# A recurrence step: its cube taken from a scaled copy, and one add moved from VectorE to GpSimd

## The reference, cut to what matters

```
# layer 1, one GRU step
r = sigmoid(i_r + h_r); z = sigmoid(i_z + h_z)          # i = x @ W_ih, h_ = h @ W_hh
n = tanh(i_n + r * h_n)
h = (1 - z) * n + z * h
# layer 2, one step of four Runge-Kutta stages, driven by x + h
dq = q - q**3 / 3 - p + drive + tanh(q) @ coupling.T + bias
dp = EPSILON * (q + ALPHA - BETA * p)
# stages at q, q + DT/2*dq1, q + DT/2*dq2, q + DT*dq3; then
q = clip(q + DT/6 * (dq1 + 2*dq2 + 2*dq3 + dq4)); p = clip(...)
```

## Time and profile before

| | |
|---|---|
| median of 3 runs | 3523.38 us (3521.14 to 3523.52) |
| the profiled execution | 3529.05 us, span 3527.2 us |
| PE busy, PEld busy | 3439.5 us, 3178.9 us |
| DVE busy | 2816.7 us (80%) |
| ACT busy | 2605.1 us (74%) |
| POOL busy | 1478.5 us (42%) |
| granted clock of TensorE, mean over the span | 0.987 of full speed |

### The profile page before, as it was taken

How to read it: one execution, slowest core, us unless ns; L and a number is a source line. 1 busy time by engine, 2 the same in 40 slices (tenths; PEclk the granted TensorE clock), 3 DMA queues, 4 the chain that set the end, 5 groups by cost and what they waited for, 6 DMA issues and landing times.

```text
span 3527.2 us, 296053 instructions
## 1 busy us (share of the span) xinstructions
PE 3439.5 (98%) x115469; PEld 3178.9 (90%) x115469; DVE 2816.7 (80%) x20699; ACT 2605.1 (74%) x23713; POOL 1478.5 (42%) x6169
## 2 busy tenths in 40 slices
PE   8989999999999999999999999999999999999978
PEld 4479999999999999999999999999999999999954
DVE  2068888888888888888888888888888888888876
ACT  3257777777777777777777777777777777777752
POOL 0024444444444444444444444444444444444421
PEclk9999999999999999999999999999999999999978
DMA  3000000000000000000000000000000000000001
GB/s 131 24 26 1 1 1 1 1 1 1 1 1 1 1 1 1 1 1 1 1 1 1 1 1 1 1 1 1 1 1 1 1 1 1 1 1 1 1 2 48
DMA packets 9433, 24.29 MB, mean 7 GB/s; under 512 B 556, under 2 KB 600, under 8 KB 8792
## 3 DMA queue, kind: packets, MB, share of 16 engines
q1 hardware_dynamic: 8832, 19.92, 1.6%
q10 hardware_dynamic: 88, 0.02, 0.0%
HBM read 15.75 MB, written 4.19 MB: 6 GB/s over the span
## 4 chain that ended last, share of the span: by engine, by line
PE 85%; DVE 7%; ACT 6%; issue 2%; DMA 0%; ACTq 0%; DVEq 0%; POOL 0%; POOLq 0%
PE psum L1187 46%; PE psum L1144 32%; PE psum L1114 5%; ACT tpart L583 2%; PE psum L1290 1%; ACT tfull L585 1%; DVE psum L895 1%; DVE tpart L852 1%; ACT qterm L558 1%; ACT pterm L554 1%; DVE psum L875 1%; DVE qnext L895 1%; DVE psum L887 0%; ACT qterm L547 0%; DVE wih L981 0%
## 5 line engine op out<-in xcount | busy, mean ns | idle before, releaser
L1187 PE MATMUL psum<-tpart,cpl 128*128 128x32 f16 (+1 forms) x65536 | 1966.8, 176 | 21.1 <-DVE tpart L852 14.5
L1187 PEld LDWEIGHTS psum<-tpart,cpl 128*128 128x128 f16 x65536 | 1781.8, 96 | 113.0 <-DVE tpart L852 22.8
L1144 PE MATMUL psum<-hpart,whh 128*128 128x32 f16 x49152 | 1553.3, 177 | 15.9 <-DVE hpart L828 12.0
L1144 PEld LDWEIGHTS psum<-hpart,whh 128*128 128x128 f16 x49152 | 1374.4, 96 | 38.3 <-DVE hpart L828 14.2
L852 DVE TENSOR_TENSOR tpart<-tfull,tpart 128x8 f16<-128x8 f32 x4096 | 682.1, 167 | 154.0 <-ACT tfull L585 11.4
L895 DVE TENSOR_REDUCE psum<-psum 128x8 f32<-128x24 f32 x3072 | 574.8, 188 | 110.1 <-PE psum L1187 3.7
L583 ACT ACTIVATE tpart<-psum 128x8 f16<-128x8 f32 x3072 | 527.3, 172 | 90.5 <-DVE psum L895 18.4
L585 ACT ACTIVATE tfull<-psum 128x8 f32<-128x8 f32 x3072 | 526.4, 172 | 0.0
L583 ACT ACTIVATE tpart<-qnext 128x8 f16<-128x8 f32 x1024 | 213.5, 208 | 312.4 <-DVE qnext L895 312.4
L505 ACT ACTIVATE rz<-gates 128x16 f32<-128x16 f32 x1024 | 241.1, 235 | 267.5 <-DVE gates L787 267.0
L547 ACT ACTIVATE qterm<-psum 128x16 f32<-128x16 f32 x3072 | 413.6, 202 | 0.0
(11 more groups left out here) (153 smaller groups left out, 4449.8 us busy)
## 6 DMA issues: line engine op xcount, KB each, us to landing
xrow<-in_x_dram SPq DMA_DIRECT2D x4, 1024.0 KB, 11.7
out_dram<-space SPq DMA_DIRECT2D x16, 256.0 KB, 2.0
wih<-in_L_cond_W_ih_dram SPq DMA_DIRECT2D x3, 1024.0 KB, 10.2
space<-in_L_cond_W_hh_dram SPq DMA_DIRECT2D x1, 3072.0 KB, 19.1
space<-in_L_cond_coupling_dram SPq DMA_DIRECT2D x1, 1024.0 KB, 19.3
xrow<-in_cond_dram SPq DMA_DIRECT2D x1, 1024.0 KB, 4.7
wih<-in_L_cond_Wk_dram SPq DMA_DIRECT2D x1, 1024.0 KB, 5.7
wih<-in_L_cond_Wo_dram SPq DMA_DIRECT2D x1, 1024.0 KB, 7.9
```

The lines of the kernel that those rows point to most:

```text
L1144: mm = pe.matmul(gate_out[x][:, :, :, c * B:(c + 1) * B], whh[:, w, k, n * P:(n + 1) * P], copies_in(hpart[:, k, :, :]), start=(c == 0 and ...
L1187: mm = pe.matmul(stage_out[a][:, 0:reps, :, col:col + B], cpl[:, w, k, n * P:(n + 1) * P], copies_in(tpart[:, s % 2, k, :, :])[:, 0:reps, ...
```

## The change

Two things are changed.

1. In stages 1 to 3 the cube's factor q is no longer read from the argument `qt` in PSUM but from one of ScalarE's scaled copies of it in `qterm` (the copy with index COPY_OF); the scale is divided out in `base`. ScalarE makes that copy first, then the square, then the other copies. The reduce that overwrites `qt` in stages 1 and 2 gets a wait for the last of the copies. Stage 0's cubic loses its wait for q1, which an earlier instruction on VectorE has already awaited.
2. `new_h_full` leaves VectorE. GpSimd makes the same add in `whole_h`: half 0 after `next_x1` and before `next_uhat`, half 1 between `pn` and `phat`. `h_low` on VectorE waits for it through `hs_ready`. On VectorE `sum_gates(1)` is moved ahead of `base(2)`.

```diff
--- before.py
+++ after.py
@@ -58,6 +58,9 @@
             lin((-1, p3), (1 / DT, q[0])),
             lin((-1, p4), (-2 / DT, q[0]), (2 / DT, q[1]), (4 / DT, q[2])),
             pn]
+
+
+COPY_OF = [2, 3, 3]
 
 
 HALVES = 2
@@ -377,11 +380,24 @@
                 pool.tensor_tensor(kept[:, x, :], rz[:, x, HC:2 * HC], hs[:, (v - 1) % 2, x * HC:(x + 1) * HC],
                                    ALU.mult).then_inc(kept_ready[x], 1)
 
+            def whole_h(x, v):
+
+                pool.wait_ge(fresh_ready[x], v)
+                pool.wait_ge(kept_ready[x], v)
+                if v > 2:
+                    pool.wait_ge(h_ready, v - 2)
+                if v > 1:
+                    pool.wait_ge(h_parts[x], v)
+                pool.tensor_tensor(hs[:, v % 2, x * HC:(x + 1) * HC], fresh[:, x, :], kept[:, x, :],
+                                   ALU.add).then_inc(hs_ready[x], 1)
+
             for x in range(HALVES):
                 keep_part(x, 1)
+                whole_h(x, 1)
             next_x1(1, 0)
             for x in range(HALVES):
                 keep_part(x, 2)
+                whole_h(x, 2)
             next_uhat(1)
             first_drive(1)
 
@@ -408,6 +424,8 @@
                                        ALU.add).then_inc(sums_ready[s], 1)
                     if s == 1 and tail <= T:
                         next_x1(tail, now)
+                        if gru <= T:
+                            whole_h(0, gru)
                         next_uhat(tail)
                     if s == 2 and gru <= T:
                         keep_part(1, gru)
@@ -416,6 +434,8 @@
                     pool.wait_ge(qterm_ready[3], now)
                     pool.wait_ge(sums_ready[2], now)
                     pool.tensor_tensor(pn[:, :], sums[:, 3, :], qterm[:, 3, 3, :], ALU.add).then_inc(pn_ready, 1)
+                    if gru <= T:
+                        whole_h(1, gru)
                     pool.wait_ge(pn_ready, now)
                     pool.tensor_scalar(phat[:, :], pn[:, :], clampc[:, 0:1], clampc[:, 1:2],
                                        ALU.min, ALU.max).then_inc(phat_ready, 1)
@@ -541,11 +561,12 @@
 
             sums_of = recovery_sums()
 
-            def stage_terms(s):
-
-                for r in range(s + 1, 4):
+            def stage_terms(s, rs):
+
+                for r in rs:
                     ins = act.activation(in_halves(qterm[:, s + 1, r, :]), qt, ACT.Copy, scale=STEP[s] * sums_of[r][s + 2])
-                ins.then_inc(qterm_ready[s + 1], 1)
+                    if r == s + 1:
+                        ins.then_inc(qterm_ready[s + 1], 1)
 
             def first_terms(v):
 
@@ -589,11 +610,13 @@
                         if s == 2 and a == 0 and gru <= T:
                             scaled_omz(1, gru)
                     if s < 3:
-                        stage_terms(s)
+                        stage_terms(s, [COPY_OF[s]])
                     arg, s_next = (in_halves(qnext[:, :]), 0) if s == 3 else (qt, s + 1)
                     if s < 3 or tail <= T:
                         act.activation(in_halves(sq[:, s_next, :]), arg, ACT.Square,
                                        scale=k_stage[s]).then_inc(sq_ready[s_next], 1)
+                    if s < 2:
+                        stage_terms(s, [r for r in range(3, s, -1) if r != COPY_OF[s]])
                     if s == 0:
                         if t >= 1:
                             plain_q(t - 1)
@@ -814,12 +837,6 @@
                     dve.tensor_tensor(part_of(x, 0), in_k(fresh[:, x, :]), in_k(kept[:, x, :]),
                                       ALU.add).then_inc(hi_ready[x], 1)
 
-            def new_h_full(x, v):
-
-                if v > 2:
-                    dve.wait_ge(h_ready, v - 2)
-                dve.tensor_tensor(hs_of(x, v), fresh[:, x, :], kept[:, x, :], ALU.add).then_inc(hs_ready[x], 1)
-
             def h_low(x, v):
 
                 if v > 0:
@@ -843,7 +860,6 @@
                 for x in range(HALVES):
                     weigh(x, v)
                     new_high(x, v)
-                    new_h_full(x, v)
                     h_low(x, v)
 
             def split_tanh(s, a, v, ready, n):
@@ -867,13 +883,14 @@
 
                 if s == 0:
                     dve.wait_ge(sq_ready[0], v - 1)
-                    dve.wait_ge(q1_ready, v)
                     dve.scalar_tensor_tensor(cub, sq[:, 0, :], CLAMP * CLAMP, q1[:, :], ALU.min, ALU.mult).then_inc(cub_ready, 1)
                 else:
 
                     dve.wait_ge(sq_ready[s], v)
-                    dve.scalar_tensor_tensor(in_halves(cub), in_halves(sq[:, s, :]), LINEAR[s], qt,
+                    dve.scalar_tensor_tensor(cub, sq[:, s, :], LINEAR[s], qterm[:, s, COPY_OF[s - 1], :],
                                              ALU.add, ALU.mult).then_inc(cub_ready, 1)
+
+            sums_of = recovery_sums()
 
             def base(s, v):
 
@@ -884,7 +901,8 @@
                                              ALU.mult, ALU.add).then_inc(base_ready, 1)
                 else:
                     dve.wait_ge(sums_ready[s - 1], v)
-                    dve.scalar_tensor_tensor(stage_base, in_halves(cub), -STEP[s - 1] / 3, in_halves(sums[:, s - 1, :]),
+                    dve.scalar_tensor_tensor(stage_base, in_halves(cub), -1 / (3 * sums_of[COPY_OF[s - 1]][s + 1]),
+                                             in_halves(sums[:, s - 1, :]),
                                              ALU.mult, ALU.add).then_inc(base_ready, 1)
 
             def sum_stage(s, a, v):
@@ -892,6 +910,8 @@
                 dve.wait_ge(stage_mm[s][a], v)
                 if a == 0:
                     dve.wait_ge(base_ready, stage_count(s, v))
+                    if s in (1, 2):
+                        dve.wait_ge(qterm_ready[s], v)
                 dve.tensor_reduce(qt[:, a, :] if s < 3 else qnext[:, a * HC:(a + 1) * HC],
                                   stage3[a].rearrange("p s c -> p c s")[:, 0:HC, :],
                                   AX.X, ALU.add).then_inc(stage_sum[s][a], 1)
@@ -936,11 +956,10 @@
                 split_tanh(2, 1, now, tanh_ready[1][1], now)
                 if gated_step:
                     new_high(0, gru)
-                    new_h_full(0, gru)
                 cubic(2, now)
-                base(2, now)
                 if gated_step:
                     sum_gates(1, gru)
+                base(2, now)
                 if gru < T:
                     h_low(0, gru)
 
@@ -958,8 +977,6 @@
                 base(3, now)
                 if gated_step:
                     new_high(1, gru)
-                    new_h_full(1, gru)
-
                 sum_stage(3, 0, now)
                 if gru < T:
                     h_low(1, gru)
```

## The result

The changed kernel takes 3416.48 us (median of 4 runs, 3412.34 to 3417.99) against 3523.38: a ratio of 0.9696, 95% interval 0.9685 to 0.9708, or 107 us less. The forecast was 3390, its range 3335 to 3450, its chance of faster .88. The profiled execution took 3417.76 us (span 3416.0), 111.3 less than the one before, or .218 for each of the 510 steps with gates; the forecast was .26.

The account below looks back on a forecast made before the run. TensorE's holes, waiting on VectorE and ScalarE chains, were taken as the bound. Savings .02 + .11 + .10 + .05 = .28 us a step, less .02 contention, times 510 gave 133 us: 3390 against the median, range 3335 to 3450.

Parts of the forecast that it names:

- TensorE is not the bound, its holes are: TensorE, shown 98% busy, issues nothing for about .6 us of every step, waiting on chains of VectorE and ScalarE.
- the five holes of .55: Late starts of TensorE's blocks before stages 0 to 3 and stage 2's gates' block, .55 us of a 6.15 step.
- the .02 that "remains inside the block": In each stage TensorE's block waits some .02 us for its second half, besides the holes before blocks.
- Stage 1 and 2 (.02 + .11): Dropped wait saves .02 us before stage 1; earlier square brings the reduce .13 earlier, saving .11 before stage 2.
- contention: VectorE's cubic of stage 2 and hpart run beside a GpSimd add: .02 us a step charged, bounds nothing and .20.
- the .28 that the forecast had before contention: Sum of savings in TensorE's holes a step, .02 + .11 + .10 + .05 us.
- The cubic's operand in SBUF: Moving VectorE's cubic operand from PSUM to the SBUF copy was taken as no change in its length.
- h_low and the gates' hole (.10): h_low releases TensorE at 2006.52, before 2006.61, so the .10 us hole before stage 2's gates' block goes.
- Stage 3 (.05): TensorE's hole before stage 3 falls from .11 to .06 us, saving .05 a step.
- GpSimd's add at nothing: The full-h add on GpSimd costs nothing; turn-around .31 us, with .15 and .06 to spare before h_low.
- The third (port): Rival: exclusive GpSimd/VectorE port, add goes before hpart, .20 us a step lost, leaving .08, 3482 us; chance .05.

Follow-up runs that it names:

- run 10: Changed kernel with GpSimd's sums add of stage 1 moved ahead of new_x and keep_part(0): 3391.75 us, 0.9624.
- run 5: Changed kernel with GpSimd's next_x1 put ahead of its sums add of stage 1: 3401.32 us, 0.9643.
- run 8: Kernel before plus only the cube from the copy and ScalarE's new order, with GpSimd's stage 1 sums add ahead of new_x and keep_part(0): 3486.42 us, 0.9896.
- run 9: Control: kernel before with only GpSimd's sums add of stage 1 moved ahead of new_x and keep_part(0): 3522.24 us, 0.9997.
- run 11: Changed kernel with GpSimd's stage 1 sums add ahead of new_x and keep_part(0), and stage 3's cubic read from PSUM: 3376.4 us, 0.9579.
- Run 6: Changed kernel with the cubic of stage 3 reading qt in PSUM again: 3401.84 us, 0.9638.
- run 4: Changed kernel with sum_gates(1) put back behind base(2): 3485.94 us, 0.9888.
- part 1 alone: Kernel before plus only the cube from the copy and ScalarE's new order; adds on VectorE, sum_gates(1) behind base(2): 3518.15 us, 0.9984.
- run 3: Changed kernel with the two adds back on VectorE behind new_high, all else as changed: 3439.45 us, 0.9752.
- Run 7: Changed kernel with TensorE's loop over four steps in place of two: 3593.82 us, 1.0187.

## Why the prediction was right, and where a step failed

**TensorE is not the bound, its holes are: right.** Its busy share did not move, and the table of holes gives the time. One reading was off: the five holes of .55 use up the whole of that step (6.15 less 5.60), so the .02 that "remains inside the block" in each stage, and that the term of stage 3 carries, is not there.

**Stage 1 and 2 (.02 + .11): the holes closed as said (.045 + .122), but what followed did not move by as much.** The step said that the first reduce gains .13 "and with it tanh, the difference, and TensorE's stage 2", and then put hpart, cubic(2), base, gates and h_low ".13 earlier with the rest". That was the failed step. They hang on the second half, and the second half hangs on argument(0), which before started .11 behind GpSimd's sums add and was not touched by it:

```profile
2005.21 0.28 POOL L407 TENSOR_TENSOR sums<-sums,qterm 128x48 f32<-128x48 f32 x1
...
2005.32 0.22 DVE L798 SCALAR_TENSOR_TENSOR narg<-gated,kap,space 128x8 f32<-128x8 f32 x1
```

Argument follows the first reduce, so it came .15 earlier in the step (mean start behind the clip 2.60 before, 2.44 after); the sums add, queued on GpSimd behind new_x and kept, which wait for ScalarE, stayed (2.48 and 2.47). Argument now starts .04 ahead of it and takes .35. So hpart came only .04 earlier behind the clip (3.32 to 3.28), and .11 earlier (3.21) in run 10, where the collision is away. Runs 5, 8 and 10 show the cause by removing it; run 9 shows that in the kernel before the order on GpSimd was worth nothing. The mis-sized term is contention: .02 in the forecast, .05 inside stage 2 and up to .04 before stage 0 by the table. With both collisions away (run 11) the gain is 148 us, .29 a step, near the .28 that the forecast had before contention.

**The cubic's operand in SBUF: wrong at nothing.** I took no change because stage 0's cubic with two SBUF inputs lasts as long; but nothing runs on GpSimd beside that one. Stage 3's runs beside pn. Run 6: 20 us.

**h_low and the gates' hole (.10): right** (.108), and run 4 shows that the reordered line carries it: with the line put back the hole is there again, about .04 larger than before the change, since h_low is stretched as well. Alone, each change leaves the hole that the other fills: part 1 alone starts stage 2 .14 earlier behind the clip (3.21 to 3.07) but h_low only .04 (3.93 to 3.88). That is why 6 and 67 make 107.

**Stage 3 (.05): .037.** Its start hangs on the same stretched second half; in run 10, with argument's collision away, .049 is saved.

**GpSimd's add at nothing: right.** It hid, in both halves, though it takes .21 there (not the .32 worked out from a factor of two) and took .16 on VectorE. Its share of the gain is 20 us (run 3). The rule of the Trainium skill, "SBUF — State Buffer", section "SBUF: two separate sides", of one operation blocking the other, was weighed on overlaps of the old trace and found not to hold. That reading was wrong, and the traces agree with the rule: in the three held pairs of the changed kernel and run 5 the VectorE operation ends .02 to .04 behind the end of the GpSimd one. In the overlaps of the old trace the hold could not show. There gated started .04 ahead of the multiply, and argument started .16 behind the start of it, so the multiply had ended (2007.23) long before argument's usual end (2007.42). What a hold costs is only the time by which it outlasts that usual end, .05 to .13 here and not .20.

**The chances.** None of the rivals came true as a whole. The third (port) was right in kind, at .09 instead of .20, but not in its pair: in the changed kernel the moved add starts ahead of hpart in 45 of 954 cases only, and hpart then takes .18.

Left open: before stage 0, 93 ns remain with the cubic mended, and in every second step the block starts .30 behind its difference in place of .22, at the loop's branch. Run 7 was to tell and failed by a cost of its own. What holds the gates' block of part 1 alone at 155 ns (run 8) was read from the queue, not tried apart from run 4.

## What to carry to other kernels

When a chain is made shorter on VectorE, look up what each instruction of it with two SBUF inputs will then start beside on GpSimd, and compare where the two end; an instruction that overlaps harmlessly now may be held after a shift of .1 us. In a pipeline with two halves, both have to come earlier: follow the second half to the end before you add a term for the first. And a queue's unused latency (here between cubic and base) can be worth more than the instruction you take off the queue: 68 us against 20, or about 43 against 20 without the collision that the order also avoids.

## What the runs showed of the hardware that I had not expected

A GpSimd add of two SBUF tiles can hold back a VectorE operation with two SBUF inputs, and then it holds it until the add has ended. The table counts the pairs that start at the distances given, from 400 to 3300 us of all 14 traces. "Behind the add" is the end of the VectorE operation less the end of the add.

| VectorE operation, its usual length | GpSimd add, where it starts | cases | held length | behind the add |
|---|---|---|---|---|
| argument, .22 | sums, 48 columns, .05 ahead to .045 behind | 2974 | .27 to .36 | .023 |
| argument, .22 (runs 8, 10, 11) | kept (a multiply), 8 columns, up to .04 behind | 1273 | .22 to .26 | .022 |
| weigh, .16 (run 5) | sums, 48 columns, .06 to .09 ahead | 376 | .24 to .26 | .024 |
| h_low, .15 (nearly all in run 4) | sums, 32 columns, .06 to .11 ahead | 465 | .17 to .20 | .023 |
| hpart, .16 | the moved add, 8 columns, .02 to .07 ahead | 531 | .17 to .21 | .020 |
| cubic of stage 3, .18 | pn, 16 columns, .03 ahead | 4270 | .22 to .23 | .036 |

So the cost is neither the add's length nor a matter of its width, but the time by which its end outlasts the usual end of the VectorE operation. Argument, when it starts .11 behind the 48 columns (the kernel before), takes its usual .22: the add ends .05 before it. The operation that comes first is not held: hpart with the moved add .02 behind it takes .16. In run 3, where h_low starts .01 ahead of the 32 columns, it takes .156 and the add takes .276 in place of .251. Argument, the one with a pointer operand, is held even by adds that start a little behind it. With one input in PSUM, beside the same 16 columns at the same distance, nothing changes (.179). It is not so beside phat, a GpSimd operation with one tile as input: h_low, .09 behind its start, takes .18 and ends .08 before it.

TensorE's loop of four steps waited for its own instructions 100.8 us of 2000, the loop of two 0.2, and its instruction queue moved 4.16 MB in place of .28.
